# Four subtractions of a unit's maxima, by VectorE in four places instead of by GpSimd in a row

## The reference

```python
x_n  = l2norm(x_ln) * scale
mu_n = l2norm(mu)
logits   = einsum('bnd,des->bnes', x_n, mu_n)
dispatch = softmax(logits, axis=1)                          # over the rows n
combine  = softmax(logits.reshape(B, N, E * S), axis=-1)    # over all slots
slot_in  = einsum('bnd,bnes->besd', x_ln, dispatch)
h        = gelu(einsum('besd,edh->besh', slot_in, W1) + b1)
slot_out = einsum('besh,ehd->besd', h, W2) + b2
out      = einsum('bsd,bns->bnd', slot_out, combine)
```

## Time and profile before

| | us |
|---|---|
| median of 3 runs (lowest, highest) | 1179.1 (1176.94, 1180.04) |
| the profiled execution, its own time | 1175.38 |
| span of its trace | 1173.4 |
| busy: PE, PEld | 1132.2, 1042.8 |
| busy: DVE, ACT, POOL | 805.0, 790.3, 716.5 |

### The profile page before, as it was taken

The page is one execution under the profiler, slowest core; times in us unless marked ns, Lnnn a source line. Parts: engine busy times, 40 slices in busy tenths (PEclk is TensorE's granted clock), DMA queues, the critical chain, the costliest instruction groups (busy, mean ns, idle before and its releaser), DMA issues. The chain is left out here.

```text
span 1173.4 us, 23675 instructions
## 1 busy us (share of the span) xinstructions
PE 1132.2 (96%) x8130; PEld 1042.8 (89%) x8130; DVE 805.0 (69%) x1896; ACT 790.3 (67%) x1656; POOL 716.5 (61%) x489
## 2 busy tenths in 40 slices
PE   7999999999999999999999999998999999999997
PEld 6899999999988998899999999998879889898886
DVE  6666675666676667666677765676586775777867
ACT  3666766766676666677776766664477895676565
POOL 5867767657774765688676676540166764556431
PEclk9999999999999999999999999999999999999999
DMA  3341111122111111111212111100110100100002
GB/s 113 86 131 45 42 33 46 33 51 53 34 28 33 46 47 45 46 33 28 50 32 55 32 46 37 37 19 3 40 33 19 42 19 15 37 24 24 10 10 72
DMA packets 49269, 47.84 MB, mean 41 GB/s; under 512 B 13176, under 2 KB 43384, under 8 KB 48896
## 3 DMA queue, kind: packets, MB, share of 16 engines
q1 hardware_dynamic: 48864, 46.25, 15.3%
q10 hardware_dynamic: 288, 0.07, 0.0%
HBM read 24.03 MB, written 2.10 MB: 22 GB/s over the span
## 5 line engine op out<-in xcount | busy, mean ns | idle before, releaser
L597 PE MATMUL ring<-kT,qT 128*128 128x384 f32 (+5 forms) x1152 | 245.6, 349 | 4.3 <-DVE kT L917 2.4
L775 ACT ACTIVATE exps<-ring,neg_max 128x128 f32<-128x128 f32 (+7 forms) x256 | 189.4, 743 | 56.3 <-DVE neg_max L926 55.3
L792 ACT ACTIVATE exp_parts<-turned 128x512 fp32r<-128x512 f32 x192 | 114.5, 597 | 131.2 <-PE turned L614 112.2
L926 DVE CUSTOM_DVE_ANT_0 ring<-ring,hidden 128x128 f32<-128x128 f32 (+7 forms) x256 | 191.5, 769 | 16.1 <-PE ring L597 15.0
L597 PEld LDWEIGHTS ring<-kT,qT 128*128 128x128 f32 x1152 | 186.9, 190 | 15.4 <-DVE kT L917 2.8
L637 PE MATMUL mix<-exp_parts,v_parts 128*128 128x256 f32 x1152 | 183.8, 295 | 0.4 <-DVE exp_parts L944 0.4
L614 PE MATMUL turned<-ident,exps 128*128 128x128 f32 x1152 | 178.5, 273 | 4.3 <-DVE exp_parts L944 3.7
L614 PEld LDWEIGHTS turned<-ident,exps 128*128 128x128 f32 x1152 | 141.2, 141 | 22.7 <-issue 3.4
L944 DVE TENSOR_TENSOR exp_parts<-turned,exp_parts 128x512 fp32r<-128x512 f32 x192 | 131.9, 687 | 29.9 <-ACT exp_parts L792 29.8
L637 PEld LDWEIGHTS mix<-exp_parts,v_parts 128*128 128x128 f32 x1152 | 148.8, 189 | 0.6 <-DVE exp_parts L944 0.6
L1054 POOL TENSOR_TENSOR cos_part<-taken,cos_sb 128x1024 f32<-128x1024 f32 (+1 forms) x39 | 93.0, 2385 | 91.4 <-ACT taken L743 91.4
(11 more groups left out here) (242 smaller groups left out, 2179.9 us busy)
## 6 DMA issues: line engine op xcount, KB each, us to landing
rotated<-taken SPq DMA_DIRECT2D x76, 256.0 KB, 3.7
raw_q<-in_L_attn_Wq_dram SPq DMA_DIRECT2D x32, 128.0 KB, 3.6
raw_o<-in_L_attn_Wo_dram SPq DMA_DIRECT2D x32, 128.0 KB, 3.3
ffn_mu_next<-in_L_ffn_mu_dram SPq DMA_DIRECT2D x28, 128.0 KB, 2.6
y_sb<-in_L_attn_x_dram SPq DMA_DIRECT2D x4, 512.0 KB, 5.8
exps_and_mu<-in_L_ffn_mu_dram SPq DMA_DIRECT2D x1, 2048.0 KB, 8.3
ffn_w_sb<-in_L_ffn_W_dram SPq DMA_DIRECT2D x8, 256.0 KB
ffn_w_sb<-in_L_ffn_W_dram SPq DMA_DIRECT2D x14, 128.0 KB, 2.7
```

Source lines behind the costliest of these rows:

```text
L597: last = nc.tensor.matmul(ring_cols(item, half * BANK, piece), qT[:, H % QUERIES, a, i * P:(i + 1) * P], kT[:, G % 2, m, half * piece:(hal ...
L775: nc.scalar.activation(dst, tile, ACT.Exp, bias=neg_max[:, H % 2, i:i + 1], scale=-1.0, accum_out=row_sum[:, H % 2, i:i + 1]).then_inc(don ...
L792: nc.scalar.activation(exp_parts[:, slot % HELD, 0, :], turned[:, n % 2, :], ACT.Copy).then_inc(done[kind], 1)
L926: nc.vector.tensor_tensor_reduce(tile, tile, later, -1.0, 3.0e38, ALU.add, ALU.min, neg_max[:, H % 2, i:i + 1]).then_inc(done[kind], 1)
```

## The change

For the units 0 to 6 the four `shift` go from POOL to DVE, each still over 1024 columns, and each gets a place of its own in the list. The first stands in step 4v+3 behind `gathered`; the second in step 4v+4 between the two `weight` on ACT, which on DVE is behind `top` and ahead of the first `combine`; the third and fourth at the end of step 4v+4, which on DVE is behind the last `combine` and ahead of the first `slot_hi`. They wait for the same semaphores and for `run` of their tile besides. Unit 7 stays as it is: its `shift` of the second half remain on POOL.

```diff
--- before.py
+++ after.py
@@ -1233,7 +1233,7 @@
         if s == 6 and sequences > 1:
             put(("vary", 1), ("std", 1, "rows"))
         if ripe and j == 0 and not last_unit:
-            put(*[("weight", v, k) for k in (0, 1)])
+            put(("weight", v, 0), ("shift", v, 1), ("weight", v, 1))
         if ripe and j == 1 and not last_unit:
             weight_parts(v, 2)
         if j in (1, 3) and live:
@@ -1249,9 +1249,10 @@
                 put(("widened_b", u))
                 if not change:
                     put(("keep", s + 1))
-                put(*[("shift", u, k) for k in range(4)])
         if j == 3 and live:
             put(("gathered", s // 2))
+            if ahead:
+                put(("shift", u, 0))
             if u:
                 fold(u + 1, 2)
                 fold(u + 1, 3)
@@ -1297,6 +1298,8 @@
                     put(("output", v, 1))
         if s == 6 and sequences > 1:
             deviations(1)
+        if ripe and j == 0 and not last_unit:
+            put(("shift", v, 2), ("shift", v, 3))
         if s + 4 < total:
             put((f"mu_load{s % 2}", s + 4))
         if j != 3:
@@ -1988,6 +1991,13 @@
                     ks = slice(2 * pair, 2 * pair + 2)
                     nc.vector.tensor_tensor(slots[:, 1, ks, 0:D], small_at_item(("output", v, pair)).rearrange("p (k d) -> p k d", k=2),
                                             slots[:, 0, ks, 0:D].bitcast(F32), ALU.subtract).then_inc(done[kind], 1)
+                if kind == "shift" and which[0] < UNITS - 1:
+                    v, k = which
+                    dve.wait_ge(done["widened_a"], v + 1)
+                    dve.wait_ge(done["widened_b"], v + 1)
+                    dve.wait_ge(done["keep"], v * UNIT + k + 1)
+                    dve.wait_ge(done["run"], v * UNIT + k + 1)
+                    nc.vector.tensor_tensor(kept(v, k), kept(v, k), peak_wide[:, :], ALU.subtract).then_inc(done[kind], 1)
                 if kind == "shift_last":
                     v, k = which
                     dve.wait_ge(done["widened_a"], v + 1)
@@ -2101,13 +2111,13 @@
                     nc.gpsimd.tensor_tensor(tile, tile,
                                             row[:, :].rearrange("p (a d) -> p a d", a=1).broadcast_to([P, 2, D]), op
                                             ).then_inc(done[kind], 1)
-                if kind == "shift":
+                if kind == "shift" and which[0] == UNITS - 1:
 
                     v, k = which
                     pool.wait_ge(done["widened_a"], v + 1)
                     pool.wait_ge(done["widened_b"], v + 1)
                     pool.wait_ge(done["keep"], v * UNIT + k + 1)
-                    cols = slice(BANK if v == UNITS - 1 else 0, N)
+                    cols = slice(BANK, N)
                     nc.gpsimd.tensor_tensor(kept(v, k)[:, cols], kept(v, k)[:, cols], peak_wide[:, cols], ALU.subtract).then_inc(done[kind], 1)
 
 
```

## The result

The changed kernel takes 1192.2 us (median of 4 runs, 1190.0 to 1197.2), the kernel before on the same chip 1178.8: the ratio is 1.0133, with a 95% interval from 1.0114 to 1.0153. It is slower. The forecast was 1192.2 in a range from 1184 to 1198. The profiled execution is the slowest of the four: 1197.16, its span 1195.4.

A forecast was written before the change was run, and what follows sets the result against it. PE was taken as the bound, delayed by DVE's order; unit losses 0.4 + 9.0 + 3.4 + 0.3 = 13.1 us on the profiled 1175.4 gave 1188.5, plus 3.7 to the median: 1192.2 us, range 1184 to 1198.

The forecast's parts named there:

- What bounds, and what the relief of POOL is worth to ACT: Expert stage: PE bounds; taking 28 subtractions off POOL by itself gives PE nothing, as ACT is late for other reasons.
- The price of one subtraction: On DVE's queue: one subtraction over 1024 columns takes 1.15 us, up to 1.9 beside POOL.
- The first and second place cost nothing: Units 0 to 6: DVE idles behind both, cost 0; the second alone up to 0.5 us late in five units.
- The third and fourth place: Ahead of the slots: two subtractions (2.3 us) plus POOL's split of mu (0.7) make DVE's copy 3.0 us late, delaying PE.
- Unit 1: PE's gather comes at once behind its other work and DVE's row is tight: 3.0 us lost.
- Unit 2: PE already waited 0.65 us for DVE's copy ahead of the gather: 3.0 us lost.
- Units 4 and 5: DVE idles 0.32 us before the copy and 0.95 before its next reading of PE: 1.7 us lost each.
- the alternative without POOL's split of mu: If that split slips in elsewhere, the 0.7 us falls away: 2.3 in three units, 1.0 in two, total 9.0 us.
- Unit 0: A shorter running maximum and an earlier maximum ahead of it give back 2.64 of 3.0 us: 0.4 us lost.
- rival 3: The lock was the bound: unit 0's exp wait, slow clock and gather wait go, 3.6 us gained, 1175.5; chance 0.14.
- Rival 1, the clock: PE's clock falls in the new waits of units 1 to 3, 1.6 us each: loss 16.7 us, 1195.8; chance 0.2.
- The other signs: Gathers in units 1 to 3 wait 7 to 11 us, running maxima all 1.23, DVE's idle gone, no gain for ACT.

The follow-up runs named there:

- Experiment 2: Kernel before with only the third and fourth subtraction of units 0 to 6 moved to DVE, first and second left on POOL: 1194.1 us, ratio 1.0147 to the kernel before.
- Experiment 1: Kernel before with only the first and second subtraction moved to DVE, third and fourth left on POOL: 1196.8 us, ratio 1.0166 to the kernel before.
- experiment 3: Kernel before, all subtractions on POOL, plus two idle 128x1024 maxima on DVE at the change's third and fourth place: 1199.7 us, ratio 1.0192.
- experiment 5: Changed kernel with the third and fourth subtraction put ahead of the running maximum, in DVE's idle time: 1177.7 us, ratio 1.0002 to the kernel before.
- the change's second trace: Profile of the changed kernel run once more, unaltered, in a later run: 1191.6 us, ratio 1.0127 to the kernel before.
- experiment 4: Changed kernel with the four small row-length instructions of unit 2 ahead of the third and fourth subtraction: 1194.1 us, ratio 1.0146 to the kernel before.

## Why the prediction was right, and where it was not

- *What bounds, and what the relief of POOL is worth to ACT*: right. POOL's 67 us went, and in units 0 to 6 no wait of ACT or PE for a subtraction was there to go with them.
- *The price of one subtraction*, 1.15 us: right; alone it is a row of 1.23. The pair at the third and fourth place takes 2.90, as 2.3 plus the turn of POOL's split (forecast 3.0), in units 0 to 3; 2.5 to 2.6 in units 4 to 6.
- *The first and second place cost nothing*: right in the main. Experiment 2 loses as much without them. But the reason was incomplete: they are free because POOL is out of the way. Experiment 1 keeps two of POOL's in, and a unit loses 2.2 us even where it has no slow stretch. And the lateness behind the second subtraction, which I estimated at 0 to 0.5 and took to be swallowed by the next place, does reach PE: 0.3 to 0.7 us at a spread in units 1, 2, 4, 5 and 6. In units 1 and 2 it is swallowed, in units 4 to 6 it is a third to two thirds of the loss.
- *The third and fourth place*: right, and the point of the whole. Two idle instructions there (experiment 3) lose the time with nothing moved, and the same two subtractions a few instructions earlier in the queue (experiment 5) lose none in units 1 and 2, and little in the others. The step on which the sum rests, the copy 3.0 us late and the gather waiting 2.6, is 2.8 and 2.5 in unit 3, and the loss there 2.9 in the change's second trace.
- *Unit 1, 3.0 forecast, 2.6 measured in every trace of the change*: 0.65 at the spread and 1.95 at the gather, whose own wait is 1.88, under the 2.6 to 3.6 that I gave as a sign.
- *Unit 2, 3.0 forecast, 6.5 measured*: the step that was mis-sized. I counted the lock only for instructions of two SBUF operands and full width. Two instructions on 8 columns stood still behind the subtractions, for 4.5 us together where experiment 4 and the kernel before have them at 0.9; that is the 3.5 us missing.
- *Units 4 and 5, 1.7 each, measured 1.0*: the number is near, the path was another. PE's gathers there don't wait at all. About 0.4 us comes earlier, at the spread behind the second subtraction (PE waits 0.26 and 0.20 us for a combine), and 0.6 later, at the spread that waits for DVE's last split (0.74 and 0.83 us). That the alternative without POOL's split of mu gave 1.0 too is luck.
- *Unit 0*: 0.4 forecast, 0.1 in one trace and 2.8 in the other. The wait for the exp (1.57 to 0.88) and the slow clock behind it (1.6) are gone as rival 3 said, and the new wait of 2.8 at the gather takes it all back. The slow stretch at that wait in the first trace costs 2.7 more.
- *Rival 1, the clock*: its mechanism occurs, its price only in part. More than one fall of PE's clock was among the signs that I would be wrong, and the first trace has three in the stage: they cost 3.6 us of its 18.1 (2.7 in unit 0 and 0.9 in unit 3, against the second trace, and nothing in unit 2). The second trace has one, in unit 2, at no price. The runs of the change differ along with it: 1197.2, 1194.1, 1190.3 and 1190.0 us at a mean clock of 0.985, 0.989, 0.993 and 0.993. Of the 5.6 us between the two profiled executions of the change 2.2 are in attention, which the change leaves alone.
- *The other signs*: PE's gathers in units 1 to 3 wait 11.0 us, the top of the 7 to 11 given; no gain in ACT's waits, right. DVE's idle time before the maximum in unit 3 fell from 1.55 to 0.31 and isn't gone, and two running maxima aren't at 1.23. The sum for the case without POOL's split of mu, given as 9.0, adds up to 8.9.
- The sum of 13.1 against 13.3 timed on the first chip, and 13.7 with the repetition, is therefore in part luck: unit 2 was 3.5 too low, units 4 and 5 together 1.4 too high, unit 1 0.4 too high, and the traces themselves say 14.7 for the seven units.

The Trainium skill's rule (SBUF — State Buffer, "Who interferes with whom") also says that `copy` and `tensor_scalar` can enter a two-port mode, if their operands meet its conditions, and that an instruction in such a mode contends with GpSimd in the same way. The 2.32 and 2.14 us above are `tensor_scalar`, and they agree; in which mode they ran, no trace shows. I had read the rule for tensors of two operands alone, and so gave these two no price.

Left open: what sets off a fall of the clock at one wait and not at an equal one, and how often the kernel before has its slow stretch in unit 0.

## What to carry to other kernels

Work that is moved to an engine with time to spare costs what it delays in that engine's queue, not what it takes: the same 28 instructions cost 13 us with 14 of them ahead of a copy that PE awaits, and nothing on balance with those 14 in an idle stretch a few instructions earlier. Look for the engine's idle rows and put the work right behind the last instruction whose result somebody waits for. And before giving a place a price, list what the other of two engines that lock each other out does at that moment, short instructions included.

## What the runs showed of the hardware

- DVE and POOL lock each other out for whole instructions, short ones too: an instruction on 128x8 took 2.32 us beside POOL's split of the weights and 0.17 without it; another took 2.14 beside that split and 0.70 beside the short one of mu. Each ended within 0.05 us behind the end of POOL's. Of queued instructions each engine gets its turn: two subtractions with one of POOL's (0.74 alone, its record 1.57) between them took 2.90.
- The granted clock fell to 0.50 at a wait of PE of 2.80 us in one execution of the changed kernel and stayed at 1.00 in another of the same program at the same place (2.78). A fall in attention, with the same instructions, came in some executions and not in others. What a fall cost differed by place: 2.7 us in unit 0, 0.9 in unit 3, nothing in unit 2, where PE waited for other engines next.
